# Cross-attention and mixture of experts on one core: weighted sums of V in groups of eight heads every eight slots instead of four every four

## What is computed

```
def _L0_xattn_ref(q, k, v, wq, bq, wk, bk, wv, bv, wo, bo):
    qp = q @ wq.T + bq
    kp = k @ wk.T + bk
    vp = v @ wv.T + bv
    ...
    scores = jnp.einsum('bhsd,bhtd->bhst', qh, kh) / jnp.sqrt(jnp.float32(D_K)).astype(qh.dtype)
    attn = jax.nn.softmax(scores, axis=-1)
    ctx = jnp.einsum('bhst,bhtd->bhsd', attn, vh)
    ctx = ctx.transpose(0, 2, 1, 3).reshape(B, S, D_MODEL)
    return ctx @ wo.T + bo
...
x = x + _L0_xattn_ref(_layernorm(x, axis=-1), ctx_1024, ctx_1024, L0_xattn_wq, ...)
x = x + _L0_ffn_ref(_layernorm(x, axis=-1), L0_ffn_Wg, L0_ffn_W1, ...)
```

## Time and profile before

| | |
|---|---|
| median of 3 runs | 1504.5 us (1492.26, 1504.5, 1509.11) |
| the profiled execution's own time | 1507.64 us |
| its span, first to last instruction | 1505.9 us |
| mean granted TensorE clock over the span | 0.936 |
| PE busy | 1301.9 us (86%) |
| DVE busy | 1072.9 us (71%) |
| ACT busy | 841.6 us (56%) |

### The profile page before, as it was taken

One profiled execution on the slowest core, in us unless ns is written; L12 is line 12 of the kernel. 1 busy time (PEld: TensorE's weight loads), 2 busy tenths in 40 slices (PEclk: granted clock), 3 DMA queues, 4 the chain that ended last, 5 costly groups with the idle time before them and its releaser, 6 DMA issues. The chain is left out here.

```text
span 1505.9 us, 34471 instructions
## 1 busy us (share of the span) xinstructions
PE 1301.9 (86%) x11773; PEld 964.6 (64%) x11802; DVE 1072.9 (71%) x2951; ACT 841.6 (56%) x1766; POOL 503.8 (33%) x592
## 2 busy tenths in 40 slices
PE   2579889999999999999885199898999899999997
PEld 1246556565665665666553078787877787888886
DVE  6667877778788888888764566665766575767664
ACT  2346757666677676777563155454555454555553
POOL 3111134422244332234222423333333343443443
PEclk9779999889999999999896599999999999999999
DMA  3866645575556665564511654344343434333333
GB/s 119 203 99 115 121 108 133 122 135 100 128 132 131 142 141 108 138 138 104 97 45 57 191 130 96 69 61 103 61 105 57 103 60 106 58 61 60 65 61 53
DMA packets 100061, 154.88 MB, mean 103 GB/s; under 512 B 14528, under 2 KB 86208, under 8 KB 94656
## 3 DMA queue, kind: packets, MB, share of 16 engines
q1 hardware_dynamic: 74032, 117.84, 35.6%
q0 software_dynamic: 25872, 35.01, 13.7%
HBM read 87.10 MB, written 65.18 MB: 101 GB/s over the span
## 5 line engine op out<-in xcount | busy, mean ns | idle before, releaser
L742 DVE TENSOR_REDUCE maxes<-s_bank 128x2 f32<-128x512 f32 x512 | 346.6, 685 | 113.5 <-PE s_bank L586 107.4
L641 ACT ACTIVATE expo<-st_bank 128x512 f32<-128x512 f32 x512 | 299.0, 598 | 70.3 <-PE st_bank L601 67.8
L74 PE MATMUL h_bank<-f_xt_hi,w 128*128 128x256 bf16 x1088 | 298.2, 274 | 8.4 <-issue 6.4
L75 PE MATMUL h_bank<-f_xt_hi,w 128*128 128x256 bf16 x1088 | 298.0, 274 | 0.0
L76 PE MATMUL h_bank<-f_xt_lo,w 128*128 128x256 bf16 x1088 | 297.9, 274 | 0.0
L586 PE MATMUL s_bank<-stack 65*128 65x256 bf16 x1024 | 204.5, 283 | 41.4 <-DVE maxes L742 36.5
L1134 POOL DMA_INDIRECT out_y<-y_out,f_token x136 | 215.4, 1584 | 26.2 <-issue 15.6
L601 PE MATMUL st_bank<-stack 67*128 67x256 bf16 x1024 | 204.0, 282 | 14.4 <-DMA stack<-negmax 10.9
L1256 ACT ACTIVATE y_out<-y_sum,gate 128x256 f32<-128x256 f32 x136 | 61.7, 500 | 241.8 <-DVE y_sum L1348 241.8
L1133 POOL TENSOR_TENSOR f_hold<-f_ones 128x1 f32<-128x1 f32 x136 | 64.0, 470 | 380.8 <-ACT y_out L1256 380.8
L1290 DVE SCALAR_TENSOR_TENSOR act_f<-h_bank,b,silu 128x256 f32<-128x256 f32 x272 | 126.2, 481 | 90.4 <-ACT silu L1226 88.9
(11 more groups left out here) (191 smaller groups left out, 2451.2 us busy)
## 6 DMA issues: line engine op xcount, KB each, us to landing
stack<-qk_scratch SPq DMA_DIRECT2D x256, 128.0 KB, 5.4
rows<-expert_rows SPq DMA_DIRECT2D x69, 260.0 KB
qk_scratch<-qk SPq DMA_DIRECT2D x32, 512.0 KB, 2.9
w_in<-in_w_units SPq DMA_DIRECT2D x8, 1536.0 KB
x<-in_x SPq DMA_DIRECT2D x16, 512.0 KB, 8.1
ctx_in<-in_ctx SPq DMA_DIRECT2D x16, 512.0 KB
out_y<-x SPq DMA_DIRECT2D x32, 256.0 KB, 2.4
expert_rows<-padding SPq DMA_DIRECT2D x9, 260.0 KB, 7.6
```

The lines of the kernel that those rows point to most:

```text
L74: pe.matmul(out, lhs_hi, rhs_hi, start=first, stop=False)
L75: pe.matmul(out, lhs_lo, rhs_hi, start=False, stop=False)
L641: act.activation(expo[:, s % E_RING], st_bank[s % 2][:], ACT.Exp, scale=SCALE).then_inc(exp_done, 1)
L742: dve.tensor_reduce(maxes[:, t, h0:h0 + 2], s_bank[r % 2][:], AX_X, ALU.max).then_inc(max_done, 1)
```

## The change

A group now holds eight heads: sixteen matmuls instead of eight, first the four heads that fill half 0 of `pv_bank`, then the four of half 1. It is issued every eighth slot, at u = 1, 9, 17, 25; the groups of slots 5, 13, 21 and 29 are gone and their work stands in the next of these. The matmuls themselves, their operands and their number are the same. The ring of exponentials has 12 slots instead of 8 (24 KB instead of 16 KB in each partition), and the waits on `pv_done` and `sums_ready` count groups of eight. `copy_sums` stays in its slots. The scratch tile `in_pad` of the tables now lies in `xn`, the normalised x.

```
-E_RING = 8
+E_RING = 12
+GROUP = 8
...
-        in_pad = sb("in_pad", [P, MAX_TILES + 1], F32)
+        in_pad = xn[:, 0, 0:MAX_TILES + 1]
...
             def weighted(v):
 
-                b, i = divmod(v, 4)
-                pe.wait_ge(exp_done, 4 * v + 4)
-                if i == 0:
+                b, half = divmod(v, 2)
+                pe.wait_ge(exp_done, GROUP * v + GROUP)
+                if half == 0:
                     pe.wait_ge(*free(("values", b // 2, b % 2)))
-                if i % 2 == 0 and v:
-
-                    pe.wait_ge(sums_ready, v // 2)
-                for c in range(2):
-                    for g in range(4):
-                        s = (4 * v + 2 * c + g // 2) % E_RING
-                        ins = pe.matmul(pv_bank[32 * g:32 * g + 32, i % 2, :], vals[b % RING][:, c, 4 * i + g, :],
-                                        expo[:, s, g % 2, :], start=c == 0, stop=c == 1, tile_position=(0, 32 * g))
+                if v:
+
+                    pe.wait_ge(sums_ready, v)
+                for i in range(2):
+                    for c in range(2):
+                        for g in range(4):
+                            s = (GROUP * v + 4 * i + 2 * c + g // 2) % E_RING
+                            ins = pe.matmul(pv_bank[32 * g:32 * g + 32, i, :],
+                                            vals[b % RING][:, c, 4 * (2 * half + i) + g, :], expo[:, s, g % 2, :],
+                                            start=c == 0, stop=c == 1, tile_position=(0, 32 * g))
                 ins.then_inc(pv_done, 1)
...
-                    v, rest = divmod(q * SLOTS + u - 5, 4)
-                    if rest == 0 and 0 <= v < NB * SLOTS // 4:
+                    v, rest = divmod(q * SLOTS + u - GROUP - 1, GROUP)
+                    if rest == 0 and 0 <= v < NB * SLOTS // GROUP:
                         weighted(v)
...
-                    act.wait_ge(pv_done, (s - E_RING) // 4 + 1)
+                    act.wait_ge(pv_done, (s - E_RING) // GROUP + 1)
...
-                act.wait_ge(pv_done, 2 * g + 2)
+                act.wait_ge(pv_done, g + 1)
...
-            table(dve.tensor_reduce(in_pad[:], ended[:], AX_X, ALU.add), 15)
+            table(dve.tensor_reduce(in_pad, ended[:], AX_X, ALU.add), 15)
```

More of the change, by code:

```diff
@@ L958, in _ @@
                                            in1=tile_row[:], op0=ALU.mult, op1=ALU.add), 17)
-            table(dve.scalar_tensor_tensor(out=tile_row[:], in0=in_pad[:], scalar=float(EXPERTS * REGION),
+            table(dve.scalar_tensor_tensor(out=tile_row[:], in0=in_pad, scalar=float(EXPERTS * REGION),
                                            in1=tile_row[:], op0=ALU.mult, op1=ALU.max), 18)
```

## The result

The changed kernel takes 1531.1 us (median of 4 runs, 1528.3 to 1534.8) against 1500.6 before (4 runs): ratio 1.0205, 95% interval 1.0137 to 1.0272. It is slower, on the side and by about the amount that was forecast (1536, range 1500 to 1549); whether by more or less than 2% the interval leaves open.

A forecast was written before the change was run, and what follows sets the result against it. Neither TensorE nor DVE alone bounds the attention; the lead changes sides within a step. Profiled 1507.6 + 7 (longer steps) + 36 (13 clock falls at 2.8) - 14 (four long steps' existing loss) gave 1536 us, range 1500 to 1549.

The forecast's parts named there:

- A step at full clock: Attention step with granted clock 1.00: goes from 44.4 to 44.9 us, +7 us over 14 steps.
- the walk: Slot-by-slot account of one attention step, TensorE and DVE early or late at each slot; ends 0.5 us late.
- rival 2: Every group's entry and exit: saved drains count fully, 14.7 us, so 1493, or 1479 without long steps; chance 0.12.
- The clock falls in every step: Thin stretch from slot 2 to slot 7's transposes grows from 3.0 to 5.7 us; clock falls, 36 us over 13 steps.
- The price of a fall: Fall hitting slots 7 to 10, 6.8 us at half clock: costs 2.8 us, bounds 0 and 3.4.
- The second kind of fall: After the picks, 3.4 us at half clock: 1.4 us of a long step's loss, left as it is.
- Rival 3: DVE starves behind four double groups a step, 0.6 us each, 34 us: 1536 to 1570; chance 0.10 without clock falls.
- Rival 1: Clock falls in the steps stay as rare as before: 1515, or 1500 if no long steps come; chance 0.25.
- The wait of 1.49 us: TensorE's row_scores of slot 29 waiting for DVE's picks; called the longest wait within a step.
- the long steps: Four profiled steps of about 48.0 us with clock falls, each losing 3.6 us against 44.4; 14 us subtracted.
- the forecast's own range: Whole kernel's time if the forecast that the clock falls in most steps holds: 1522 to 1549 us; chance 0.53.

The follow-up runs named there:

- the kernel with three of them: Kernel before with ring of 12, groups of slots 13, 21 and 29 issued late at 17, 25 and 1 (three double groups): 1485.6 us, ratio 0.9886.
- the changed kernel with filler: Changed kernel plus five useless bf16 matmuls behind row_scores of slot 5 (eight in the text on record): 1498.5 us, ratio 0.9965 to the kernel before.
- the kernel with 21 and 29: Kernel before with ring of 12, groups of slots 21 and 29 issued late at 25 and 1: 1489.3 us, ratio 0.9857.
- the four runs with filler: Runs of the kernel before plus useless matmuls, three at slot 4 and five at slot 28: 1492.9 us, ratio 0.9894.
- the one with only slot 5 late: Kernel before with ring of 12, only slot 5's group issued late, at slot 9 before that slot's own: 1534.8 us, ratio 1.0221.

## Why the prediction was right

The mechanism was right and each main term can be read off; the point forecast (1536) is 5 us above the median. That the ratio came so close (1.0205, forecast 1.021) is in part luck: the sum started from a profiled execution of 1507.6 us, 7 above the later median of 1500.6, and added 29 us, where the two profiled executions differ by 22.0 and the two medians by 30.5.

- **A step at full clock.** Forecast 44.9 us, measured 44.81 where the clock holds. The stations of the walk came out within 0.1 us, and slot 16's row_scores wait 0.67 us where about 0.8 was said. The plain gain of the drains (rival 2, 44.37 less four times 0.23) did not appear. A double group took 1.93 us by the row against 1.95 expected.
- **The clock falls in every step.** Forecast so for 13 steps, and found: 6.8 us at 0.50 in each of twelve regular steps. Shown as cause by two experiments from opposite sides: taking only slot 5's group away brings the falls (and the whole loss), filling slot 5 in the changed kernel removes them.
- **The price of a fall.** Forecast 2.8, measured 2.97 us. TensorE leads in the slots it hits, so little of the 3.4 is hidden. This is what a fall costs in these regular steps; whether it is a price that would hold in a step of another length no run shows (see the last section).
- **The second kind of fall,** after the picks, I left "off and on". It does not appear in the regular steps of the changed kernel: each has one fall. The attention grew by 26 us where 29 were summed, and the experts, of which nothing was forecast, took 4 us less in this one profile.
- **Rival 3** (bursts starve DVE) had for it the 2.64 us wait. But that wait stands where the clock is low; at full clock DVE waits 0.71 us behind the same double group and 0.5 us more in a whole step than before, and the kernel with three of them is faster than the one before. The rival's own sum comes to 1535 for its low end (1507.6 + 7 + 34 - 14), not 1536.
- **Rival 1** (falls as rare as before) is what the changed kernel with filler does, 1498.5: the rival's price, 1500 to 1515, was fair; its condition was not met.
- **Loose places.** The wait of 1.49 us is not the longest within a step: the earlier trace rows has 1.8 us for a weight load. The saved drains alone (1493) are 0.8% under 1504.5, so the 0.10 that rival 2 got for a gain of over 1% hung on the long steps vanishing too. The 1522 of the forecast's own range is not worked out anywhere.

Two rules stood on the two sides. That a change of tiling mode drains TensorE (the Trainium skill, "TensorEngine Tiling (Array Packing)", Key Properties) agrees with late issue at slot 21, where TensorE leads: in the kernel with 21 and 29 the steps' picks come 0.79 us earlier, 0.56 of it won at slots 29 to 1 and 0.23 at 21 to 25, just the drain that was worked out. That idle gaps between bursts are what to avoid (the Trainium skill, "TensorE: Matmul & The Clock Gate", Why this matters for your kernels) does not cover this case: the clock fell behind 6.8 us in which TensorE was busy for 5.13, and no wait in them was longer than the 0.59 us before the transposes of slot 3.

## What to carry to other kernels

When two engines hand the lead to each other within a period, price a moved piece of work at both ends: it is worth its length only where its engine leads at the slot it leaves, and costs its length where its engine leads at the slot it joins. Look at what stays behind as well: a stretch in which TensorE is only partly busy can lose the clock once its last solid burst is taken out, and the loss falls on the dense work that follows. If such a stretch can't be filled with real work, matmuls whose result nobody reads can pay, as long as they stand where TensorE waits anyway.

## What was not expected

Eight useless matmuls a step made the kernel before 1% faster (0.9894) and its runs alike: 2.7 us between the slowest and the fastest of 4, where the kernel before had 22 in 13. That the scatter of the kernel before is how much clock it loses is borne out by the granted clock of its runs: of the 25 runs the four with a clock of 0.946 or more took 1489.8 to 1494.1 us, the six with 0.931 or less 1502.9 to 1514.5; the four runs with filler had 0.949 or 0.950. In which steps it was lost was read off one profile of each alone.

The changed kernel and the one with only slot 5 late have the same step of 47.79 us to 0.01, though the second has three more drains and slots 13, 21 and 29 at their old places. The kernel before has it too: its falls of 6.8 us in the long steps are 47.79 us apart, this one following the one at 277.53 of the earlier trace rows,

```profile
325.32:332.15 6.83, 6.35 (x38) 0.50 1.00 200
```

while its picks there were 47.98, 47.90 and 47.84 apart. The time between two falls seems to set the step once each step has one; that is a reading of three traces, not shown by an experiment. What fixes that length was not tried and stays open; so does why one kernel's falls come in every other step.
